# VectorE folds the head products of blocks 0 and 1, GpSimd folds block 3 a second time and clears the value buffer earlier

## The reference, cut to what matters

```python
k_ = v_ = ctx.reshape(B, H, head_dim, L)          # B 8, H 16, head_dim 8, L 256
kv = jnp.einsum('bhil,bhjl->bijhl', k_, v_)       # 8 x 8 products per head
y  = causal convolution of kv with ssm_kernel along l
out = y + kv * D
out = jnp.einsum('bijhl,bhil->bjhl', out, q_)     # times q, summed over i
x = x + tanh(g_xattn[0]) * out
x = x + tanh(g_ffn[0]) * ffn0(layernorm(x))       # router, top 8, low rank and base projection
...                                               # second layer: attention, mixture of experts
```

## Time and profile before

| what | value |
|---|---|
| median of 3 runs | 190.18 us (189.53 to 190.3) |
| the profiled execution | 190.67 us, of which the span from first to last instruction is 188.8 us |
| TensorE busy | 170.0 us, 90% of the span |
| VectorE busy | 153.0 us, 81% |
| ScalarE busy | 113.6 us, 60% |
| GpSimd busy | 94.6 us, 50% |
| the chain that ended last | TensorE 61%, ScalarE 16%, DMA 7%, VectorE 7%, issue 4% |

### The profile page before, as it was taken

How to read it: one execution, slowest core, us unless ns; L and a number is a source line. 1 busy time by engine, 2 the same in 40 slices (tenths; PEclk the granted TensorE clock), 3 DMA queues, 4 the chain that set the end, 5 groups by cost and what they waited for, 6 DMA issues and landing times.

```text
span 188.8 us, 3740 instructions
## 1 busy us (share of the span) xinstructions
PE 170.0 (90%) x1204; PEld 115.2 (61%) x1204; DVE 153.0 (81%) x463; ACT 113.6 (60%) x293; POOL 94.6 (50%) x157
## 2 busy tenths in 40 slices
PE   7989999998999999989579879978989899999981
PEld 7957666667665555556356656655658557655640
DVE  0789989984599989989999999979874997748644
ACT  2465034833342446753699899998799796652630
POOL 1079999994999331510643306333304569294000
PEclk9999999999999999999999999999999999999998
DMA  5979976100000000000000000000000097875953
GB/s 162 330 213 354 382 316 239 68 0 3 0 2 0 0 2 0 3 0 0 0 3 2 0 3 2 3 0 3 0 0 3 17 177 90 166 131 106 174 149 111
DMA packets 22770, 15.18 MB, mean 80 GB/s; under 512 B 17664, under 2 KB 21344, under 8 KB 22368
## 3 DMA queue, kind: packets, MB, share of 16 engines
q1 hardware_dynamic: 22112, 13.94, 27.9%
q10 hardware_dynamic: 640, 1.02, 1.6%
HBM read 9.68 MB, written 1.07 MB: 57 GB/s over the span
## 4 chain that ended last, share of the span: by engine, by line
PE 61%; ACT 16%; DMA 7%; DVE 7%; issue 4%; SPq 2%; DVEq 0%
PE PS L1801 9%; ACT R L745 6%; PE PS L1434 5%; DMA CT<-ctxr 5%; PE PS L1431 5%; PE PS L1430 5%; PE PS L1535 4%; ACT R L740 4%; PE PS L1819 4%; PE PS L1648 4%; PE PS L1505 4%; PE PS L1469 3%; PE PS L1632 3%; PE PS L1457 3%; DMA R<-R 3%
## 5 line engine op out<-in xcount | busy, mean ns | idle before, releaser
L1116 DVE TENSOR_REDUCE SM<-PS 128x8 f32<-128x1024 f32 x16 | 18.9, 1216 | 2.0 <-PE PS L1618 1.8
L1632 PE MATMUL PS<-CON,R 128*128 128x128 f32 x128 | 18.4, 276 | 1.4 <-ACT R L745 1.3
L354 POOL TENSOR_TENSOR R<-CT 128x512 f32<-128x512 f32 (+1 forms) x16 | 16.0, 1001 | 6.4 <-DMA CT<-ctxr 6.4
L541 POOL TENSOR_SCALAR R<-QT,SM 128x256 bf16<-128x256 f32 x32 | 16.0, 517 | 5.9 <-DVE SM L1195 5.6
L745 ACT ACTIVATE R<-PS 128x512 f32<-128x512 f32 x32 | 18.4, 606 | 0.2 <-PE PS L1632 0.2
L1317 DVE TENSOR_TENSOR R<-R,PS 128x512 bf16<-128x512 f32 (+1 forms) x17 | 11.7, 686 | 7.6 <-PE PS L1801 5.6
L1801 PE MATMUL PS<-R 128*128 128x512 bf16 x64 | 16.4, 379 | 0.8 <-DMA R<-R 0.8
L496 POOL TENSOR_TENSOR R<-R,ROW 128x256 f32<-128x256 f32 x8 | 5.8, 737 | 21.6 <-ACT R L682 10.9
L550 POOL TENSOR_TENSOR R<-R 128x640 f32<-128x640 f32 (+1 forms) x12 | 15.0, 1284 | 2.8 <-DVE T_R L1045 2.8
L1632 PEld LDWEIGHTS PS<-CON,R 128*128 128x128 f32 x128 | 14.3, 140 | 3.1 <-issue 2.7
L883 ACT ACTIVATE R<-PS 128x512 f32<-128x512 f32 x17 | 10.1, 595 | 9.7 <-PE PS L1801 9.5
(11 more groups left out here) (168 smaller groups left out, 447.0 us busy)
## 6 DMA issues: line engine op xcount, KB each, us to landing
WST<-w SPq DMA_DIRECT2D x3, 1024.0 KB, 12.7
T_R<-lagged SPq DMA_DIRECT2D x2, 768.0 KB, 7.7
X<-x SPq DMA_DIRECT2D x2, 512.0 KB, 4.9
CT<-ctxr SPq DMA_DIRECT2D x2, 512.0 KB, 8.3
y<-X SPq DMA_DIRECT2D x8, 128.0 KB, 2.0
WQP<-wqp ACTq DMA_DIRECT2D x1, 512.0 KB, 7.1
WKV<-wkv SPq DMA_DIRECT2D x1, 512.0 KB, 10.0
R<-sw SPq DMA_DIRECT2D x3, 128.0 KB, 4.3
```

Of the source, the lines that this page charges most:

```text
L354: return eng.tensor_tensor(KV[:, h % RING, lo:hi, 0:32].rearrange("p c (i j) -> p c i j", i=4), k[:, :, 0:4].unsqueeze(3).to_broadcast([P, ...
L541: nc.gpsimd.tensor_scalar(XB[:, u % XS, j, :], MX[:, b, :], GG[:, b, e:e + 1], 1.0, ALU.mult, ALU.mult).then_inc(e_xb, 1)
L1116: V_.tensor_reduce(MX1[:, b % 2, 8 * c:8 * c + 8], S4[:, 8 * c:8 * c + 8, :], AX.X, ALU.max, negate=True).then_inc(a_mx, 1)
L1632: ins = TR(PS[:, 4 + k % 2, P * h:P * h + P], SS[:, b % 2, 4 * k + h, :], I)
```

## The change

VectorE gets an instruction of its own kind, `fold_first`, which does for blocks 0 and 1 what `fold_sums` does for the others: after head 11 the heads 0 to 9 of block 0, after head 13 those of block 1, and after head 15 the heads 10 to 15 of both. `turn_sums` of these blocks then takes 4 terms, 8 matrix instructions, and waits on the new semaphore `fold_v`. On GpSimd `FOLD1` becomes 3, so block 3 is folded a second time as well; the two MEMSETs move ahead of the wait on `f_z`; and the second folds are spread among the first ones.

```diff
-        FOLD1 = 4
+        FOLD1 = 3
...
             for b in range(FOLD0, NB):
                 fold_sums(b, 0, FOLD_H)
+            pool.wait_ge(conv, NH0)
+            nc.gpsimd.memset(V[:, :, :, 16:17], 1.0).then_inc(v_ones, 1)
+            nc.gpsimd.memset(V[:, :, :, 17:VW], 0.0).then_inc(v_ones, 1)
             for b in range(FOLD0, NB):
                 if b == FOLD0:
                     pool.wait_ge(f_z, 1)
                 fold_sums(b, FOLD_H, NH0)
-                if b == FOLD0 + 3:
-                    pool.wait_ge(conv, NH0)
-                    nc.gpsimd.memset(V[:, :, :, 16:17], 1.0).then_inc(v_ones, 1)
-                    nc.gpsimd.memset(V[:, :, :, 17:VW], 0.0).then_inc(v_ones, 1)
-            fold_again(FOLD1)
-            fold_again(FOLD1 + 1)
+                if b >= FOLD0 + 3:
+                    fold_again(b - 2)
             for b in range(NB - 3):
                 bias_values(b)
-                if b + FOLD1 + 2 < NB:
-                    fold_again(b + FOLD1 + 2)
+                if b < 2:
+                    fold_again(NB - 2 + b)
...
+            def fold_first(b, lo, hi):
+
+                dve.wait_ge(prod, NPR * hi)
+                pair = PR[:, :, :, :, :].rearrange("p (a b) i h j -> p b a i (h j)", a=NL)[:, b]
+                at = slice(HD0 * lo, HD0 * hi)
+                V_.tensor_tensor(pair[:, :, 0:4, at], pair[:, :, 0:4, at], pair[:, :, 4:8, at], ALU.add
+                                 ).then_inc(fold_v, 1)
+
             for h in range(NH0):
                 units_of(h)
+                if h in (11, 13):
+                    fold_first((h - 11) // 2, 0, FOLD_H)
                 if h == 7:
...
             assert pr.n == PREP
+            fold_first(0, FOLD_H, NH0)
+            fold_first(1, FOLD_H, NH0)
...
             def turn_sums(b):
 
-                if b == 0:
-                    pe.wait_ge(prod, NPR * NH0)
-                if b >= 2:
+                terms = 4
+                if b < FOLD0:
+                    pe.wait_ge(fold_v, FOLD0 + b + 1)
+                else:
                     pe.wait_ge(x1, b - 1)
-                terms = 8
-                if b >= FOLD0:
                     pe.wait_ge(fold, NB - FOLD0 + b - FOLD0 + 1)
-                    terms = 4
                 if b >= FOLD1:
                     pe.wait_ge(fold_more, b - FOLD1 + 1)
                     terms = 2
```

More of the change, by code:

```diff
@@ L236, in build @@
         fold_more = sem("fold_more")
+        fold_v = sem("fold_v")
         prod = sem("prod")
```

## The result

The changed kernel takes 199.78 us (median of 4 runs, 199.63 to 199.96), the kernel before 190.24 us beside it (4 runs, 189.53 to 190.46): a ratio of 1.051, 95% interval 1.048 to 1.0538. Slower was forecast, at 192.2 us. The loss is more than four times the forecast 2.0 us.

What follows compares the result with a forecast made beforehand. The chain was taken to run over TensorE's transposes of blocks 0 and 1. Sums starting +3.16 us later, -0.92 for fewer transposes and -0.2 gave +2.0; 190.18 + 2.0 = 192.2 us, range 189.8 to 194.6.

Steps and rivals of the forecast that it cites:

- the price of block 0's first addition: Stage one, behind head 11: VectorE's 128x640 addition waits only for GpSimd's first fold and ends at 37.99, about 1.5 us.
- Block 1's addition: Stage one, behind head 13: asked at 41.03, 0.16 us too late, it waits until 42.38 and ends at 43.09.
- TensorE's convolution is not held up: End of stage one: heads 14 and 15 end 2.6 us later on VectorE, but TensorE's head 15 needs only head 12's products.
- Rival 2: TensorE's clock falls in its 3.9 us pause before the sums; 5 us at half rate loses 2.5 us: 194.7 us, chance 0.16.
- Rival 1: Block 1's addition slips in between two folds, its second half meets the sixth; first transposes at +1.3: 191.5 us, chance 0.14.
- Rival 3: VectorE's additions are not held, all four adding up to at most about 2.5 us: 189.7 us, chance 0.14.
- Rival 4: Stage two gives 1 to 3 us back, folds ending earlier and VectorE's routes running free: 189 us or less, chance 0.08.
- the forecast's bounds of -0.44 and +1.28: Stage two: -0.44 us if TensorE's path saves block 3's transposes, +1.28 if VectorE pays the whole added fold; zero taken.
- the smaller terms: Around the folds and sums: 640 elements end 0.71 us after release, GpSimd loses 0.57 us, 16 transposes take 1.84 us.

Runs made afterwards that it cites:

- the run with 30 matrix instructions: Changed kernel plus 30 idle TensorE matrix instructions (ones by ones, into an unread bank) ahead of head 15: 198.09 us, ratio 1.0437 to the kernel before.
- the kernel with five waits: Changed kernel, but GpSimd waits for the end of each of its six 128x640 folds before starting the next: 192.88 us, ratio 1.0126 without the longest run.
- the kernel with one gap behind the first fold: Changed kernel plus one GpSimd wait on its own first fold, ahead of the second; folds two to six unbroken: 195.06 us.
- the version whose additions meet no fold, with block 0 alone: Kernel before, but VectorE folds block 0 behind heads 11 and 15, GpSimd waiting for it before its first and fifth folds: 189.18 us, ratio 0.9969.
- the last version: GpSimd steps aside for both blocks: VectorE's first halves behind heads 9 and 10, GpSimd's second folds as in the kernel before: 192.33 us, ratio 1.0142.

## Why the prediction was wrong, and where it was right

**The step that failed** is the price of block 0's first addition: "GpSimd's first fold holds until 35.77 + 1.51 = 37.28, so the addition ends at 37.99". It was asked for when forecast (36.01; the stage ran 0.43 us earlier in this execution, so 36.44 against 36.50) and took 9.00 us instead of 1.5. It had to wait not for a fold but for the whole run. The rows on which the step rested couldn't show that: the fold met at 50.58 was the last before the MEMSETs, and the products at 12 us are of another form. No row there has a VectorE instruction inside a run of equal folds. The trace before has one in stage two (53.70 for 0.73 us, inside the two 128x384 folds from 53.35 to 55.31), and it got in at the end between them: it would have spoken for the step that failed, so stage two's ends were no guide to stage one's. The upper bound was in plain sight, the end of that run (44.83, plus 0.7 us), and was not taken into the range.

**What hung on it** went the other way. Block 1's addition was to meet a fold and take 2.06 us; the run was over, and it took 0.81. "TensorE's convolution is not held up" was wrong: head 15 does need only head 12's products, but these were behind the addition, and TensorE waited 7.21 us.

**The sum.** The first `f_x1` was forecast at 47.63, 47.20 with the 0.43 us taken off, and came at 53.94, 6.7 us later: +7.5 us for the first addition, -1.2 for the second, and +0.46 that VectorE waited for TensorE's head 15 at half rate. The profiled execution is 7.3 us above its 192.7: these 6.7, less the 0.43 by which the stage ran earlier, less 0.1 to the end of the span (stage two gave back 0.3, the rest of the span lost 0.2), and 1.1 outside it (199.96 - 197.0 = 2.96 us, before 190.67 - 188.8 = 1.87).

**Rival 2** happened beside it, but one step earlier than it said: the long pause stood ahead of head 15, which the forecast had on time, and not between TensorE's small work and the sums (there it was 1.31 us). Its price of 2.5 us wasn't right either: head 15 lost 1.8 us, and the run with 30 matrix instructions shows 0.5 us of it on the path. The 5 us at half rate came from the opening, where the clock column of the earlier trace rows reads 1.00 all the same, so those rows don't show that the clock set the rate there. The Trainium skill, TensorE: Matmul & The Clock Gate, section HAM oscillation, warns of waits between bursts; the 0.50 inside the pause of 7.21 us and right behind that of 3.31 us agrees.

**Rival 1** is what the kernel with five waits did, within 0.1 us in its shortest run (1.4 us of loss against 1.3); its median is 3.4 us above the kernel before, the clock having fallen in the traced run. **Rival 3** (not held) fell, with 10.8 us for the four additions against its bound of 2.5. **Rival 4** fell: stage two gave back 0.3 us, not 1 to 3, inside the forecast's bounds of -0.44 and +1.28.

**Right** were the smaller terms. An addition of 640 elements ended 0.68 us after release (0.71 forecast). GpSimd lost about 0.6 us to each addition that got in (10.20 us for six folds with two additions between them, 8.99 without; forecast 0.57). Sixteen transposes took 1.94 us (1.84), the time from the first of them to `f_x1` was 1.10 us (1.06) and from there to the next transposes 2.16 us (2.11). The MEMSETs held nobody: in the kernel with one gap behind the first fold the two second halves took 1.03 us beside them. There the rule of the Trainium skill, SBUF — State Buffer, section Who interferes with whom, agrees, as it does on large additions keeping folds out. For the 9.00 us the prediction read "the first to issue blocks the other fully" as the length of one instruction; here VectorE lost again at five ends, though it had asked before each next fold started.

**Open** is why one wait on its own fold makes GpSimd's later ends passable, why without it stage one's ends are closed while stage two's are open, and why in one stage two VectorE was kept out for 6.35 us all the same. What the idea could gain looks small: the version whose additions meet no fold, with block 0 alone, won 0.3%.

## What to carry to other kernels

Before an instruction with two SBUF inputs goes to VectorE beside a row of GpSimd's, bound its wait by the end of the whole row, and not only of the instruction under way, and look what else stands behind it in VectorE's list. If the two must share the stretch, a wait in GpSimd's list (on VectorE's instruction, or on GpSimd's own first one) brought the first addition here from 9.0 us to 1.5 or to its own 0.8. Work saved on TensorE is lost when the wait for it lowers the clock, so count the pause as well as the work.

## What was not expected of the hardware

One wait of GpSimd on its own fold, early in a run of six, changed who wins at the later ends: 1.48 us against 5.85 us for the same addition in the third fold, with no gap near either.

The time outside the span isn't constant. In 51 runs of the kernel before that stood beside the experiments it was 1.8 to 2.0 us. In the changed kernel it was 2.7 to 3.0 in four runs, and it went up to 3.0 in some runs of most kernels with a long pause of TensorE, among them four of six of the last version, where the clock hadn't fallen. In all eight runs with TensorE kept busy it was 1.8 to 1.9 us. The profile shows nothing of what lies there, so the cause stays open.
